# Token rows normalised and split before their transposition, one gate product, gate weights spread by select products, one return step

## The chip, the cores and the metric

The kernel runs on 1 core of one Trainium2 chip. The metric is the device time of one execution in microseconds (us); lower is better. The engines of a core are TensorE (PE: products; PEld: its weight loads), VectorE (DVE), ScalarE (ACT), GpSimd (POOL) and SyncE (SP, which here only issues transfers).

## The reference, cut to what matters

64 images of 3 x 224 x 224 and 64 texts of 77 x 64 are embedded, joined and sent through one attention block and one mixture of experts:

```python
h = patches @ W_embed + b_embed + positions            # 784 patches of 8x8, 64 features
for i in range(3):                                      # grid graph: own node plus four neighbours
    hw = h @ W_gcn[i]
    h = relu(normalised_adjacency @ hw + b_gcn[i])
h = concat([h @ W_out + b_out, txt], axis=1)            # 861 tokens
h = h + attn(layernorm(h))                              # 4 heads of 16; its output rounded to bfloat16 before Wo
h = h + ffn(layernorm(h))

def ffn(x):
    all_out = experts_mlp(x)                            # 4 experts: 64 -> 128 -> 64 -> 64, relu
    shared = shared_mlp(x)                              # 64 -> 64 -> 128 -> 64, relu
    gates = softmax(x @ gW + gb)                        # 4 gates
    topv, topi = top_k(gates, 2); topw = softmax(topv)
    return shared + sum(all_out[topi] * topw)
```

## The kernel before

**Tiling.** An image is 861 tokens = 7 blocks of 123 (`BLK`); `PIECES` are the first four and the last three blocks (492 and 369 columns), `HALVES` two times 432 columns. Two images make a pair: embedding and graph run per pair with both images side by side, attention and experts per image.

**Order.** Nothing is scheduled at run time. Each image and each pair is a list of steps such as `("s", g, half, kb, h)`; `spread` gives each step of a list a due time between a start and an end, in proportion to `COST`, and one unit of due time is one image. The constants `MAX`, `FINISH`, `NORM_M`, `EXPERT`, `NORM_A`, `PROJECT`, `VALUE` (even image, odd image), `GRAPH` and `PACK` (pair) place the lists against each other. All steps of 16 images, sorted by due time, make one window; each engine walks through the same sorted list and does its own part of every step, in that order, waiting on semaphores. The windows are separated by a drain of all engines. So a step that an engine can't start holds up all that stands behind it on that engine.

**Banks.** Steps in `ROTATING` take PSUM banks 0, 1, 2, 3, 6, 7 in turn. PE may fill a bank when the step six turns before has been read out of it. Banks 4 and 5 hold the attention output (`pv`).

**The steps that matter here**, for image g:
- `s` (L969, 56 an image): scores, read out by ACT as exponentials (L678). `pv` (L978, 14): probabilities times values, four products into four 32-column strips of the array.
- `mx` (L990, 56): scores the other way round, read out by DVE as row maxima (L790). `mrow` (L995, 2): maxima transposed, copied by ACT, sent to `QS` by SP (L559).
- `ln`, `ln2`, `ln3` (`a` before attention, `m` before the experts): layer norm on DVE, with the square on ACT and the power -0.5 on POOL. `ln3` writes the normed rows twice (L854, L855).
- `xt` (L1032): both copies of the normed rows transposed by PE; ACT rounds all 128 rows into `XS` (L694), then DVE subtracts the rounded value in rows 64 to 127 (L860), so that `XS` holds high part over low part. `qk`, `l1` (L1043), `v` and `gate` (L1054) multiply `XS` by the high and low parts of the weights.
- `gate`, `g2`, `g3`: gate values, softmax, top two, weights `GW`. In `g3` ACT repeats each weight over 64 columns (L736) into `GWW`; `wb` (L1091, 4 steps) transposes that, and DVE multiplies the hidden layer by it (L935).
- `l2` (L1083 for experts, L1081 for the shared one), `l3` (L1099), `back` (L1106, 2 steps): the result in two halves of 64 partitions goes back to token rows; DVE adds it to `H` in `OUTT` (L943), SP stores it (L565).
- `hb`: POOL adds the bias rows to `H`.
- `gw` (L1017) and `gagg` (L1026): graph layer of a pair. ACT writes the rounded `UH` (L685), DVE the rest `UL` (L809). `QKH`/`QKL` of `qk` lie in the same two tiles.
- `load` (SP, 24 transfers, L543), `xc` (POOL, L619), `embed` (L1002): a quarter of the pair's image rows. `xc` waits for the landing, and the next `load` for `xc`.
- `stack`: ACT issues 8 transfers (L717, L718) that bring q and k of image g from scratch memory into `QS` and `KS`. Due at g - 1, so once an image.

## Time and profile before

| | |
|---|---|
| median of 3 runs | 6032.26 us (6030.95 to 6034.13) |
| profiled execution, its own time | 6031.67 us |
| span from first to last instruction | 6029.7 us |
| mean granted TensorE clock | 0.914 |
| PE busy | 89% of the span |
| DVE, ACT, POOL busy | 58%, 51%, 21% |

The span is shorter than the execution's own time by 2 us. The granted clock is a share of full speed. Busy shares are means over setup (about the first 300 us) and the loop over images.

### The profile page before, as it was taken

To read this page: it belongs to the slowest core of one execution; us is meant where nothing else is said; L and a number is where in the kernel's file an instruction comes from. 1 tells how busy PE (TensorE), PEld (TensorE's weight loads), DVE (VectorE), ACT (ScalarE), POOL (GpSimd) and SP (SyncE) were. 2 spreads that over 40 slices of the span, in tenths; PEclk is the share of its full clock that TensorE was granted. 3 is DMA by queue.
4 is the path that set the end of the run, shared out by engine and by line. 5 is a ranking of instruction groups with operands and counts; after the bars stand their busy time and mean duration, and the time that the engine had idled before them with its cause. 6 is when DMAs were issued, how large, how long until landed. Compare 5 with 4: busy or idle time off the path is not lost.

```text
span 6029.7 us, 88160 instructions
## 1 busy us (share of the span) xinstructions
PE 5341.6 (89%) x30542; PEld 3460.2 (57%) x30542; DVE 3515.4 (58%) x7398; ACT 3046.5 (51%) x6161; POOL 1255.9 (21%) x1168
## 2 busy tenths in 40 slices
PE   4488999899989898999889999989998999989997
PEld 3355665556556555665556666555665555656654
DVE  2356565666555666665566665566655566656563
ACT  0044555555555555455555455555555455555555
POOL 1111221221221222122122122122122122122212
PEclk8689999998998999999998998999999899999988
DMA  1443234324334323323323323333433433332320
GB/s 36 67 68 65 50 57 71 61 52 71 56 46 71 63 52 70 57 53 63 69 50 66 57 51 65 68 58 59 70 50 53 69 58 58 71 52 50 55 39 5
DMA packets 331182, 347.37 MB, mean 58 GB/s; under 512 B 108778, under 2 KB 280938, under 8 KB 330730
## 3 DMA queue, kind: packets, MB, share of 16 engines
q1 hardware_dynamic: 289770, 228.36, 17.6%
q10 hardware_dynamic: 40960, 113.28, 15.3%
q8 instruction: 248, 4.06, 0.3%
q14 instruction: 204, 1.67, 0.1%
HBM read 269.85 MB, written 70.73 MB: 56 GB/s over the span
## 4 chain that ended last, share of the span: by engine, by line
PE 55%; DVE 15%; DMA 9%; ACT 8%; issue 5%; ACTq 4%; SPq 1%; POOL 1%; POOLq 0%; DVEq 0%
PE ps L978 10%; PE ps L990 9%; PE ps L1026 9%; PE ps L969 7%; DVE neg_max_halves L790 7%; DMA k_stack<-qk_scratch 6%; DMA image_rows<-in_x 3%; PE ps L1043 3%; ACT probs L678 3%; PE ps L1083 3%; PE ps L1054 3%; PE ps L1099 3%; ACTq L717 2%; ACTq L718 2%; PE ps L1002 2%
## 5 line engine op out<-in xcount | busy, mean ns | idle before, releaser
L790 DVE TENSOR_REDUCE neg_max_halves<-ps 123x1 f32<-123x432 f32 (+1 forms) x3584 | 2016.9, 599 | 775.3 <-PE ps L990 762.6
L678 ACT ACTIVATE probs<-ps 123x432 f32<-123x432 f32 x3584 | 1727.9, 532 | 621.8 <-PE ps L969 607.1
L990 PE MATMUL ps<-k_stack,q_stack 96*123 96x432 f32 x3584 | 1373.2, 415 | 86.1 <-DMA k_stack<-qk_scratch 53.2
L969 PE MATMUL ps<-q_stack,k_stack 97*123 97x432 f32 x3584 | 1341.8, 416 | 63.4 <-SPq L583 24.8
L978 PE MATMUL ps<-probs,v_and_one 123*32 123x432 f32 x7168 | 908.6, 581 | 170.7 <-ACT probs L678 167.0
L990 PEld LDWEIGHTS ps<-k_stack,q_stack 96*123 96x123 f32 x3584 | 652.5, 192 | 692.7 <-issue 515.3
L969 PEld LDWEIGHTS ps<-q_stack,k_stack 97*123 97x123 f32 x3584 | 684.6, 199 | 427.5 <-issue 285.0
L1026 PE MATMUL ps<-adjacency,parts_hi 112*128 112x392 f32 x1344 | 513.4, 382 | 8.4 <-DVE parts_lo L809 4.4
L1026 PE MATMUL ps<-adjacency,parts_lo 112*128 112x392 f32 x1344 | 496.9, 370 | 0.0
L690 ACT ACTIVATE nodes_T<-nodes_T,plain_w 128x392 f32<-128x392 f32 x192 | 119.5, 623 | 699.7 <-DVE nodes_T L827 699.7
L749 ACT ACTIVATE hidden<-ps,plain_w 128x432 f32<-128x432 f32 x640 | 380.8, 620 | 93.8 <-PE ps L1043 92.8
L978 PEld LDWEIGHTS ps<-probs,v_and_one 123*32 123x32 f32 x7168 | 147.0, 112 | 427.1 <-ACT probs L678 230.5
L827 DVE TENSOR_TENSOR nodes_T<-ps,dinv_row 128x392 f32<-128x392 f32 x192 | 108.8, 567 | 485.9 <-PE ps L1026 485.9
L635 POOL TENSOR_TENSOR ln_stats_a<-ln_stats_a,minus_half 123x7 f32<-123x7 f32 x64 | 94.6, 1478 | 1355.8 <-DVE ln_stats_a L848 1355.8
L631 POOL TENSOR_TENSOR nodes_T<-nodes_T,dinv_row 128x392 f32<-128x392 f32 x128 | 136.6, 1067 | 959.3 <-ACT nodes_T L690 959.3
L619 POOL COPY patch_columns<-image_rows 96x392 f32<-96x392 f32 x256 | 237.8, 957 | 392.1 <-DMA image_rows<-in_x 374.1
L755 ACT ACTIVATE hidden<-ps,plain_w 128x492 f32<-128x492 f32 (+1 forms) x384 | 238.4, 621 | 142.4 <-PE ps L1081 127.8
L1026 PEld LDWEIGHTS ps<-adjacency,parts_hi 112*128 112x128 f32 x1344 | 283.7, 211 | 45.1 <-issue 40.4
L644 POOL TENSOR_TENSOR tokens<-tokens,bias_rows 123x448 f32<-123x448 f32 x64 | 73.4, 1147 | 1125.7 <-DVE gate_weights L928 1125.7
L809 DVE TENSOR_TENSOR parts_lo<-ps,parts_hi 112x512 fp32r<-112x512 f32 x192 | 119.8, 625 | 308.6 <-ACT parts_hi L685 308.6
L648 POOL TENSOR_TENSOR tokens<-tokens,moe_T 123x448 f32<-123x448 f32 x256 | 293.1, 1145 | 20.1
L685 ACT ACTIVATE parts_hi<-ps 112x512 fp32r<-112x512 f32 x192 | 106.3, 554 | 364.5 <-PE ps L1017 229.7
(147 smaller groups left out, 7256.9 us busy)
## 6 DMA issues: line engine op xcount, KB each, us to landing
q_stack<-qk_scratch ACTq DMA_DIRECT2D x256, 216.0 KB, 9.4
k_stack<-qk_scratch ACTq DMA_DIRECT2D x256, 216.0 KB, 10.7
image_rows<-in_x SPq DMA_DIRECT2D x768, 49.0 KB
image_rows<-in_x SPq DMA_DIRECT2D x768, 48.8 KB
image_rows<-in_x SPq DMA_DIRECT2D x768, 48.6 KB
image_rows<-in_x SPq DMA_DIRECT2D x768, 48.3 KB
qk_scratch<-parts_hi SPq DMA_DIRECT2D x64, 432.0 KB, 2.5
qk_scratch<-parts_lo SPq DMA_DIRECT2D x64, 432.0 KB, 3.5
```

The lines of the kernel that those rows point to most:

```text
L619: pool.tensor_copy(XCB[:, b, :, :].rearrange("p g (i j) -> p g i j", j=GRID), src).then_inc(xc_done, 1)
L648: ins = pool.tensor_tensor(hb, hb, TMP[:, :, :], ALU.add)
L678: act.activation(P[:, unit % 2, h, :], T[0:BLK, 0:HW], ACT.Exp, scale=SCALE).then_inc(free[r], 1)
L749: act.activation(H1[e % 3][:, c0:c0 + cn], T[:, 0:cn], ACT.Relu, bias=bias).then_inc(free[r], 1)
L755: act.activation(H2[j][:, c0:c0 + cn], T[:, 0:cn], ACT.Relu, bias=bias).then_inc(free[r], 1)
L790: v.tensor_reduce(NM[:, qb * HEADS + h, half:half + 1], T[0:BLK, 0:keys], AX.X, ALU.max, negate=True).then_inc(free[r], 1)
L969: mm = pe.matmul(T[0:BLK, 0:cn], KS[:, g % 2, h, kb * BLK:(kb + 1) * BLK], QS[:, g % 2, h, c0:c0 + cn], start=True, stop=True)
L978: pm = pe.matmul(acc[32 * h:32 * h + 32, half, 0:HW], VV[:, g % 2, kb, h, :], P[:, slot, h, :], start=kb == 0, stop=kb == NB - 1, tile_pos ...
L990: mm = pe.matmul(T[0:BLK, 0:cn], QS[0:SHIFT_ROW, g % 2, h, qb * BLK:(qb + 1) * BLK], KS[0:SHIFT_ROW, g % 2, h, c0:c0 + cn], start=True, st ...
L1026: mm = pe.matmul(T[:, 0:GHALF], part[:, k, :], adj[:, k, half * GHALF:(half + 1) * GHALF], start=k == 0 and part is UH, stop=k == NG - 1 a ...
L1043: mm = pe.matmul(T[:, 0:cn], wsplit(part, name, e, cols), XS[which][:, c0:c0 + cn], start=part is WH, stop=part is WL)
L1054: mm = pe.matmul(T[0:BLK, k * cols:(k + 1) * cols], XS[which][:, k * BLK:(k + 1) * BLK], wsplit(part, "v" if kind == "v" else "gW"), start ...
```

## The change

- `ln3` writes one normed copy, then its rounded high part and the low part into `XHL`, both on DVE and token-major. `xt` transposes `XHL` by a plain product with the rounded unit matrix `ident_r` (124 columns a block, `PITCH`), and ACT alone reads the bank out. The DVE part of `xt` is gone. One `XN` serves both norms; `ln3` waits for the last `xt`.
- `mrow` is a plain product with `ident_r` too.
- `gate` multiplies each block once by the 8 columns `gsplit` (high and low part of the gate weights side by side); DVE adds the two halves.
- `g3` no longer uses ACT. DVE splits the weights into three bfloat16 parts `GP` (5 small operations); a new step `wt` transposes them (7 transpositions in bfloat16 into 12 partitions), ACT copies them to `GT` in rows 96 to 107, and each `wb` is one product of the 12-row matrix `select` with `GT`, in the array rows from 96.
- `back` is one step: 4 transpositions of all 128 partitions, two additions of DVE in place in `H`, and the store goes out of `H`. `wo` of image g now waits for the store of image g - 2; there is a semaphore for even and one for odd images.
- The two `l2` steps of a pair of experts share one due time, and so do the four `wb` steps, so that they stand side by side in the order.
- All placing constants are new. Setup makes `ident_r`, `gsplit`, `select` and clears `OT2`.

```diff
-COST = {"s": 1, "pv": 4, "mx": 1, "embed": 5, "gw": 5, "gagg": 12, "xt": 4, "qk": 2, "v": 7, "gate": 7, "l1": 2,
-        "l2": 4, "wb": 4, "l3": 12, "ot": 4, "obt": 2, "wo": 6, "back": 2, "mrow": 4}
+COST = {"s": 1, "pv": 4, "mx": 1, "embed": 5, "gw": 5, "gagg": 12, "xt": 2, "qk": 2, "v": 7, "gate": 4, "l1": 2,
+        "l2": 4, "wt": 2, "wb": 1, "l3": 12, "ot": 4, "obt": 2, "wo": 6, "back": 4, "mrow": 2}
...
-                4: [("l2", g, 1, 0), ("l2", g, 1, 1)]}[e]
-    return out + [("wb", g, 0, 0), ("l2", g, 2, 0), ("wb", g, 0, 1), ("l2", g, 2, 1), ("wb", g, 1, 0), ("wb", g, 1, 1),
-                  ("wait", 1), ("l3", g), ("wait", 1), ("back", g, 0), ("back", g, 1)]
-MAX = ((-0.804, 0.046), (-0.666, 0.05))
-FINISH = ((0.986, 1.13), (0.995, 1.13))
-NORM_M = ((1.131, 1.265), (1.15, 1.27))
-EXPERT = ((1.357, 2.01), (1.29, 1.974))
-NORM_A = ((-1.38, -1.233), (-1.9, -1.82))
-PROJECT = ((-1.247, -1.114), (-1.76, -1.666))
-VALUE = (-0.968, -0.96)
-GRAPH = (-2.04, -1.484)
-PACK = (-3.7, -3.2, -2.653, -2.19)
-LOAD_LEAD, EMBED_LAG = 0.292, 0.07
+        out += {0: [("g2", g)], 1: [("g3", g)], 2: [[("l2", g, 0, 0), ("l2", g, 0, 1)], ("hb", g)], 3: [],
+                4: [[("l2", g, 1, 0), ("l2", g, 1, 1)]]}[e]
+    return out + [("wt", g), ("l2", g, 2, 0), ("l2", g, 2, 1),
+                  [("wb", g, 0, 0), ("wb", g, 0, 1), ("wb", g, 1, 0), ("wb", g, 1, 1)], ("wait", 1), ("l3", g), ("wait", 1), ("back", g)]
+MAX = ((-0.816, -0.01), (-0.723, 0.05))
+FINISH = ((0.994, 1.13), (1.003, 1.13))
+NORM_M = ((1.131, 1.265), (1.2, 1.258))
+EXPERT = ((1.357, 1.964), (1.301, 1.99))
+NORM_A = ((-1.38, -1.245), (-1.613, -1.533))
+PROJECT = ((-1.247, -1.114), (-1.425, -1.289))
+VALUE = (-0.978, -1.013)
+GRAPH = (-2.077, -1.521)
+PACK = (-3.956, -3.348, -2.807, -2.314)
+LOAD_LEAD, EMBED_LAG = 0.138, 0.193
...
+                        sp.dma_start(dst, H[:, :, st[1] % 2, :]).then_inc(out_dma[st[1] % 2], 16)
...
-                        act.activation(XS[st[2]][:, c0:c0 + cn], T[:, 0:cn], ACT.Copy).then_inc(xt_hi, 1)
+                        act.activation(blocked(XS[st[2]][:, c0:c0 + cn]), pitched(T[:, :], cn), ACT.Copy).then_inc(free[r], 1)
...
-                    elif kind == "g3":
-                        counted(act, g_weight, nth, st)
-                        counted(act, out_dma, ranks(steps, lambda s: s[0] == "back" and s[2] == 1), ("back", st[1] - 1, 1), 16)
-                        act.activation(GWW[:, :, :, :], GW[:, :, :].unsqueeze(3).to_broadcast([BLK, NB, EXPERTS, HID]),
-                                       ACT.Copy).then_inc(g_wide, 1)
+                        act.activation(XN[:, :, 1, :], XN[:, :, 0, :], ACT.Square).then_inc(squared, 1)
+                    elif kind == "wt":
+                        act.wait_ge(full[r], n)
+                        act.activation(GT[:, 0:TOKENS].rearrange("p (k n) -> p k n", n=BLK),
+                                       T.bitcast(BF16)[0:3 * EXPERTS, 0:NB * (BLK + 1)].rearrange("p (k n) -> p k n", k=NB)[:, :, 0:BLK],
+                                       ACT.Copy).then_inc(free[r], 1)
...
-                        v.tensor_tensor(XN[which][:, :, 1, :], XN[which][:, :, 0, :], rstd, ALU.mult)
-                        v.tensor_tensor(XN[which][:, :, 0, :], XN[which][:, :, 0, :], rstd, ALU.mult).then_inc(normed, 1)
-                    elif kind == "xt":
-                        v.wait_ge(xt_hi, hi_no[st])
-                        tile = XS[st[2]]
-                        c0, cn = PIECES[st[3]]
-                        v.tensor_tensor(tile[64:128, c0:c0 + cn], T[64:128, 0:cn],
-                                        tile[64:128, c0:c0 + cn].bitcast(F32), ALU.subtract).then_inc(free[r], 1)
+                        filled(v, turn, xt_last[st])
+                        settle(v.tensor_tensor(XN[:, :, 0, :], XN[:, :, 0, :], rstd, ALU.mult))
+                        settle(v.tensor_copy(XHL[:, :, 0, :], XN[:, :, 0, :]))
+                        v.tensor_tensor(XHL[:, :, 1, :], XN[:, :, 0, :], XHL[:, :, 0, :].bitcast(F32),
+                                        ALU.subtract).then_inc(normed, 1)
...
+                        counted(v, out_dma[g % 2], out_no[g % 2], ("back", g - 2), 16)
...
-                        ins = v.tensor_tensor(GZ[:, 0, :, :], T[0:BLK, 0:NB * EXPERTS].rearrange("p (k e) -> p k e", e=EXPERTS),
-                                              row("gb", 0, EXPERTS).unsqueeze(1).to_broadcast(sh), ALU.add)
-                        ins.then_inc(free[r], 1)
+                        t8 = T[0:BLK, 0:NB * 2 * EXPERTS].rearrange("p (k a e) -> p k a e", a=2, e=EXPERTS)
+                        settle(v.tensor_tensor(GZ[:, 0, :, :], t8[:, :, 0, :],
+                                               row("gb", 0, EXPERTS).unsqueeze(1).to_broadcast(sh), ALU.add))
+                        v.tensor_tensor(GZ[:, 0, :, :], t8[:, :, 1, :], GZ[:, 0, :, :], ALU.add).then_inc(free[r], 1)
...
+                        v.wait_ge(g_weight, nth[st])
+                        filled(v, turn, ("wt", st[1] - 1))
+                        settle(v.tensor_copy(GP[:, :, 0, :], GW[:, :, :]))
+                        settle(v.tensor_tensor(GR[:, 0, :, :], GW[:, :, :], GP[:, :, 0, :], ALU.subtract))
+                        settle(v.tensor_copy(GP[:, :, 1, :], GR[:, 0, :, :]))
+                        settle(v.tensor_tensor(GR[:, 1, :, :], GR[:, 0, :, :], GP[:, :, 1, :], ALU.subtract))
+                        v.tensor_copy(GP[:, :, 2, :], GR[:, 1, :, :]).then_inc(g_parts, 1)
...
+                        t4 = T[0:BLK, 0:4 * 128].rearrange("p (k t f) -> p k t f", t=2, f=HID)
+                        v.tensor_tensor(H[:, 0:4, g % 2, :], t4[:, :, 0, :], H[:, 0:4, g % 2, :], ALU.add)
+                        v.tensor_tensor(H[:, 4:NB, g % 2, :], t4[:, 0:3, 1, :], H[:, 4:NB, g % 2, :], ALU.add
+                                        ).then_inc(free[r], 1)
...
-                            mm = pe.transpose(T[0:HEADS, at * BLK:(at + 1) * BLK],
-                                              NMM[:, k * HEADS:(k + 1) * HEADS], ident[0:BLK, 0:BLK])
+                            mm = pe.matmul(T[0:HEADS, at * PITCH:(at + 1) * PITCH], NMM[:, k * HEADS:(k + 1) * HEADS],
+                                           ident_r[0:BLK, 0:BLK + 1], start=True, stop=True)
...
-                            src = XN[st[2]][:, k, :, :].rearrange("p a f -> p (a f)")
-                            mm = pe.transpose(T[:, at * BLK:(at + 1) * BLK], src, ident[0:BLK, 0:BLK])
+                            src = XHL[:, k, :, :].rearrange("p a f -> p (a f)")
+                            mm = pe.matmul(T[:, at * PITCH:(at + 1) * PITCH], src, ident_r[0:BLK, 0:BLK + 1],
+                                           start=True, stop=True)
...
+                            x_ = XS[which][:, k * BLK:(k + 1) * BLK]
+                            if kind == "gate":
+                                mm = pe.matmul(T[0:BLK, k * 2 * EXPERTS:(k + 1) * 2 * EXPERTS], x_, gsplit[:, :],
+                                               start=True, stop=True)
...
+                        counted(pe, g_parts, nth, ("g3", st[1]))
+                        for k in range(NB):
+                            mm = pe.transpose(T.bitcast(BF16)[0:3 * EXPERTS, k * (BLK + 1):k * (BLK + 1) + BLK],
+                                              GP[:, k, :, :].rearrange("p a e -> p (a e)"), ident_bf[0:BLK, 0:BLK])
                     elif kind == "wb":
                         _, g, j, t = st
+                        c0, cn = PIECES[t]
                         if (j, t) == (0, 0):
-                            counted(pe, g_wide, nth, ("g3", g))
-                        for k, at in blocks_of(t):
-                            src = GWW[:, k, 2 * j:2 * j + 2, :].rearrange("p a f -> p (a f)")
-                            mm = pe.transpose(T[:, at * BLK:(at + 1) * BLK], src, ident[0:BLK, 0:BLK])
+                            emptied(pe, turn, ("wt", g))
+                        mm = pe.matmul(T[:, 0:cn], select[:, 2 * j:2 * j + 2, :].rearrange("p a f -> p (a f)"),
+                                       GT[:, c0:c0 + cn], start=True, stop=True, tile_position=(SEL_ROW, 0))
...
+                        emptied(pe, turn, ("l3", st[1]))
+                        for k in range(4):
+                            mm = pe.transpose(T[0:BLK, k * 128:(k + 1) * 128], OT2[:, k * BLK:(k + 1) * BLK], ident[:, :])
```

## Rows read from the trace of the kernel before

**Rows 1.** The page: span, and busy time of each engine.
```profile
span 6029.7 us, 88160 instructions
PE 5341.6 (89%) x30542; PEld 3460.2 (57%) x30542; DVE 3515.4 (58%) x7398; ACT 3046.5 (51%) x6161; POOL 1255.9 (21%) x1168
```

**Rows 2.** Windows: length, busy us (instructions) of each engine, PEclk, DMA share, GB/s.
```profile
1500.00:4500.00 3000.00, 2732.66 (x15765) 1769.25 (x15765) 1811.55 (x3819) 1588.02 (x3214) 651.19 (x608) 0.93 0.34 59
2619.38:2627.14 7.76, 7.76 (x28) 7.31 (x28) 1.16 (x3) 1.04 (x3) 0.00 (x0) 0.50 1.07 126
```

**Rows 3.** Waits: who waited for whom, us in total, times, longest.
```profile
PE ps L978 <- ACT probs L678: 167.0, 233, 2.6
...
PE ps L1054 <- DVE parts_lo L809: 122.0, 30, 5.2
...
PE ps L990 <- DMA k_stack<-qk_scratch: 53.2, 22, 28.6
```

**Rows 4.** Timeline, two pieces a pair apart: start, length, what [idle before].
```profile
2618.25 0.49 ACT L685 ACTIVATE parts_hi<-ps 112x384 fp32r<-112x384 f32 x1 [4.28 <-issue]
...
2619.38 0.41 PE L1054 MATMUL ps<-split_hi,x_stack_attn 128*123 128x64 f32 x1 [4.15 <-DVE parts_lo L809]
...
2796.90 0.41 PE L1054 MATMUL ps<-split_hi,x_stack_attn 128*123 128x64 f32 x1 [4.16 <-DVE parts_lo L809]
```

**Rows 5.** Window of L1054 alone: fourteen gate products of one image.
```profile
3011.15:3012.65 1.50, 1.50 (x14) 1.48 (x13) 1.00 0.58 85
```

**Rows 6.** Timeline of PE around three `wb` transpositions.
```profile
3046.61 0.46 PE L990 MATMUL ps<-k_stack,q_stack 96*123 96x432 f32 x1
3046.90 0.48 PE L1091 MATMUL ps<-ident,gate_weights_wide 123*128 123x123 f32 x3
3047.14 0.44 PE L990 MATMUL ps<-k_stack,q_stack 96*123 96x432 f32 x1
```

**Rows 7.** Timeline of PE around three `back` and three `ot` transpositions.
```profile
3063.57 0.46 PE L990 MATMUL ps<-k_stack,q_stack 96*123 96x432 f32 x1
3063.95 0.53 PE L1106 MATMUL ps<-ident,moe_T 64*123 64x64 f32 x3
3064.41 0.65 PE L990 MATMUL ps<-k_stack,q_stack 96*123 96x432 f32 x2
3064.91 0.49 PE L1061 MATMUL ps<-ident,attn_T 128*123 128x128 f32 x3
```

**Rows 8.** Timeline of PE: products in bfloat16, and transpositions into 4 partitions.
```profile
56.69 1.65 PE L394 MATMUL ps<-onehot_dst,onehot_src 126*112 126x392 bf16 x9
...
2628.10 0.57 PE L1066 MATMUL ps<-ident_bf,attn_bf 123*64 123x123 bf16 x7
...
3067.43 0.48 PE L995 MATMUL ps<-ident,neg_max 123*4 123x123 f32 x3 [1.20 <-DVE neg_max L797]
3067.67 0.86 PE L969 MATMUL ps<-q_stack,k_stack 97*123 97x432 f32 x3
```

**Rows 9.** Groups by form, DVE and ACT: count, busy us, mean ns, idle.
```profile
L790 DVE TENSOR_REDUCE neg_max_halves<-ps 123x1 f32<-123x432 f32 x1792 | 1078.3, 602 | 493.6 <-PE ps L990 487.1
...
L855 DVE TENSOR_TENSOR normed_twice_m<-normed_twice_m,ln_stats_m 123x448 f32<-123x448 f32 x64 | 39.6, 619 | 0.0
...
L860 DVE TENSOR_TENSOR x_stack_moe<-ps,x_stack_moe 64x369 fp32r<-64x369 f32 x64 | 35.0, 547 | 18.5 <-ACT x_stack_moe L694 17.6
...
L928 DVE TENSOR_TENSOR gate_weights<-gate_vals,gate_sums 123x28 f32<-123x28 f32 x64 | 12.1, 189 | 2.2
...
L678 ACT ACTIVATE probs<-ps 123x432 f32<-123x432 f32 x3584 | 1727.9, 532 | 621.8 <-PE ps L969 607.1 <-issue 4.0
```

**Rows 10.** Timeline of SP and POOL: two loads, the packing after one.
```profile
2617.16 25.53 SPq L543 DMA_DIRECT2D image_rows<-in_x  x24
...
2722.16 14.09 SPq L543 DMA_DIRECT2D image_rows<-in_x  x24
...
2738.66 1.77 POOL L619 COPY patch_columns<-image_rows 96x392 f32<-96x392 f32 x2 [11.29 <-DMA image_rows<-in_x]
```

More of the change, by code:

```diff
@@ L31 @@
 BLK = 123
+PITCH = BLK + 1
 NB = TOKENS // BLK
@@ L48 @@
 SHIFT_ROW = 96
+SEL_ROW = 96
 HW = 432
@@ L195, in windows @@
     return out
-ROTATING = ("s", "embed", "gw", "gagg", "mx", "mrow", "ot", "obt", "wo", "xt", "qk", "v", "gate", "l1", "l2", "wb", "l3",
+ROTATING = ("s", "embed", "gw", "gagg", "mx", "mrow", "ot", "obt", "wo", "xt", "qk", "v", "gate", "l1", "l2", "wt", "wb", "l3",
             "back")
```

114 lines of the change are left out of this document (64 added, 50 removed).

## The prediction

> **What bounds the kernel now.** I read the page first: PE is busy 89% of the span, the next engine 58% [rows 1]. In the loop PE is busy 2732.7 of 3000 us at a granted clock of 0.93 [rows 2], so PE work saved there is time saved, unless another engine sets the pace in that stretch. A pair of images takes 2796.90 - 2619.38 = 177.5 us [rows 4], an image 88.8 us, which turns due times into us. The missing 9% is not spread evenly. The list of waits names a PE wait of 122.0 us in 30 times at the first `v` product, one a pair [rows 3]. The timeline shows its chain [rows 4]: ACT issues the 8 transfers of `stack` and is away 4.28 us ("issue"), only then evicts the second half of `gw` (L685), DVE follows, and `v`, which takes the bank of that `gw` six turns later, starts 4.15 us late. After it come 28 products, 14 of `v` and 14 of `gagg`, in 7.76 us at clock 0.50 [rows 2], which is the 1.2 GHz level after an idle PE. Two smaller stops a pair stand behind the other `stack`: `pv` waits for exponentials that queue behind it on ACT, and the first `mx` for the landing of `k_stack` [rows 3].
>
> **PE work, per image at full clock.** Because products overlap, I take ends, not lengths. Fourteen gate products take 1.50 us, 0.107 each, though only 4 columns stream: their 123-column weight load sets it [rows 5]. Three `wb` transpositions end 3047.38 - 3047.07 = 0.31 us after the product before, 0.105 each, with a run-out of 0.48 - 0.31 = 0.17 us, and the next 432-column product ends 0.20 us later [rows 6].
> - `gate`: 14 products become 7: -0.75 us.
> - `back`: 7 x 0.107 becomes 4 x 0.11 (three `ot` transpositions, the same shape, end 0.34 us apart from what precedes [rows 7]): -0.31.
> - `wb`: 14 x 0.105 = 1.47 goes. Bfloat16 streams 392 columns in (1.65 - 0.17) / 9 = 0.164 us, and seven small transpositions take (0.57 - 0.17) / 7 = 0.057 each [rows 8]. So 2 x (0.21 + 0.155) = 0.73 for the four products and 0.40 for `wt`: -0.34.
> - `mrow`: 7 transpositions at 0.105 become products of 124 columns with 4 weight columns. At the 0.20 us for 432 columns that is 0.057: -0.34. `xt`: 14 products with 128 weight columns, 0.107 x 128/123 = 0.111 against 0.105: +0.08. No row shows this rounded format streaming 65 to 391 columns. One bound is 0.057; the other is 0.22, two passes of 0.11 as an unrounded 128-column product would take by the `ot` price. Then `mrow` and `xt` cost 21 x 0.115 = 2.4 us more instead of saving 0.26. I take the lower price, as gate, `s` and `mx` are all in this format and none runs in two passes.
> - Array shape. `back` works on 64 partitions. Three of its transpositions end 0.45 us after the product before and the two products behind end 0.58 later [rows 7]: 0.45 - 3 x 0.107 = 0.13 us going in, 0.58 - 0.40 = 0.18 coming out. `pv`, `embed`, `obt`, `l2` of the experts and `l3` are strips as well. I laid out the due times of both versions for one window of 16 images: before, 24.0 entries into a strip shape and 21.9 returns an image; after, 22.5 and 19.0. Gone are two `back` and two of four `l2` entries, added one `wt`, one `wb` (the four stand together) and 1.5 `mrow`. That is 1.5 x 0.13 + 2.9 x 0.18 = -0.72.
>
> The Trainium skill, page TensorEngine Tiling (Array Packing), section Tiling Modes, says that changing the mode drains TensorE; it speaks against the new `wt`, `wb` and `mrow`, and for the grouped `l2` and `back`. The trace agrees for `back` (0.31 us in all), but `mrow` with 4 output columns shows nothing of it now: after its three transpositions three products end in 0.62 us, their plain price [rows 8]. By the rule `mrow` as a plain product pays from now on; by that row it would not, and the array-shape term would be 2.5 x 0.13 + 3.9 x 0.18 = -1.03, 20 us less in all. I take it as paying.
>
> The sum is -0.75 - 0.31 - 0.34 - 0.34 + 0.08 - 0.72 = -2.38 us an image, -152 us for 64.
>
> **The order.** In the new due times `gw` of the first layer falls at 1.953 and 1.967 of a pair, `v` at 1.987, and `stack` at 2.0. So the eviction that PE waited for now stands ahead of the 8 issues on ACT. Behind them on PE come two `gagg` (5.0 us), two `ot` and four `s`, about 6.6 us of work (a 392-column product is 0.18 us at the rate of `mx`), before `pv` needs exponentials that ACT has after 4.28 + 3 x 0.53 = 5.9 us [rows 4, 9]. The stop of 122.0 us goes, and with it the low clock: 7.76 us at 0.50 would be 3.88, 30 times 116 us. Together -238 us. The other `stack` keeps its place at 1.0 and its stops: the first `mx` is due 1 us earlier (1.184) but waits for the same landing. `ln` and its square move away from there, which frees `pv` sooner, only for `mx` to wait longer: zero.
>
> **DVE and ACT.** DVE loses four `xt` subtractions, the shorter 0.55 us, 2.4 us an image, and gains a copy in `ln3` (between 0.19 and 0.62 by [rows 9]; I take 0.35) twice, one small operation in `gate` and five in `g3` at 0.19: about -0.6. ACT loses the wide copy and gains the narrow one. Neither mean matters; the place does. `ln`, `ln2`, `ln3` of the odd image are now due at 1.387 to 1.44, in between `gate`, `g2` and `g3` of the even one. From 1.387 to 1.515, 11.4 us, DVE has 5 large operations of 0.62 (3.1), a copy (0.35), 23 small ones of 0.19 (4.4) and 9 maxima of 0.60 (5.4): 13.2 us [rows 9]. Before, a stretch as long held 11 small ones and 11 maxima, 8.7 us. Behind them on DVE stand maxima whose banks PE needs. I charge 2 us a pair, +64. Four `wb` side by side leave four reads of some 0.6 us to DVE within 0.73 us of PE; PE has two banks beyond them. I charge 0.5 us an image, +32; zero and 1.5 us are the bounds.
>
> **Transfers.** `load` now comes 0.138 (12.3 us) ahead of `xc`, before 0.292 (25.9). The packing starts 2738.66 - 2722.16 = 16.5 us after the first issue when it must wait [rows 10], so POOL will stand in `xc` some 4 us in each. Behind it on POOL is the power of `ln2` (due 0.665, `xc` 0.652), and DVE's `ln3` at 0.710 waits for that: 1 us, hidden by the banks. `load` at 1.906 stands ahead of `mrow`'s transfers of 1.963 on SP; the row is needed at 2.5. The store out of `H` is waited for by `wo` 100 us later. Setup gets six more small operations on DVE and one clearing on POOL, under 2 us, left out.
>
> The profiled execution took 6031.7 us, within 1 us of the median, so 6031.7 - 152 - 238 + 64 + 32 = 5738 us.
>
> **Rivals.**
> - *Only the products.* ACT's 4.28 us of issuing are still there, and my margin behind them was 6.6 against 5.9 us. If the stop only moves from `v` to `pv`, the order brings nothing: 6032 - 152 = 5880. For it: all engines walk one order, and what ACT holds up must be somewhere. Against it: 5 us of that margin are `gagg`, which nobody has to empty in between.
> - *Slow narrow products.* At 0.22 us each, 2.4 + 0.26 us an image more, +170: 5908. For it: no row in between. Against it: `v` streams 64 columns at the gate's pace.
> - *More than forecast.* DVE's stretch is absorbed, no charge of 96 us, and `pv` and `mx` behind the other `stack` wait 2 to 3 us a pair less: about 5560.
> - *Slower: the late load.* The load that shares its time with `stack` takes 25.53 us only to issue, the other 14.09 [rows 10]. If all did, with packing 2.4 us behind the last issue as in [rows 10] and its two copies of 1.77 us, POOL would reach the power 29.7 us after the first issue, while `ln3` is due 0.196 of an image, 17.4 us, after it. DVE would stand over 12 us, PE some 11 after its banks are full: 32 pairs x 11 = 352, 5738 + 352 = 6090. It decides from 9.2 us a pair on, a packing that starts 26 us after the first issue. Against it: only the first load of a pair meets `stack`, and nothing near it needs POOL.
>
> **How the numbers follow.** Forecast 0.52 (5640 to 5820), only the products 0.17, slow narrow products 0.07, more than forecast 0.12, late load 0.06, and 0.06 that several DVE stretches become the pace and it stays where it was. The range 5585 to 5910 takes in the first three and half of the fourth. A change below 0.2% (12 us) can't be told from none here: faster 0.89, same 0.04, slower 0.07.
>
> **What would show it.** Right: the wait of L1054 on `parts_lo` gone, granted clock of the loop above 0.95, gate products 7 an image at 0.107, `xt` at 0.11, `back` without the 0.31 us. Wrong: a PE wait at `pv` right behind the first `stack`; `mx` banks waited for around g3; POOL in `xc` over 10 us with DVE idle before `ln3`.

## The result, and the profile after

The changed kernel takes 6074.82 us (median of 4 runs, 6072.12 to 6078.07), the kernel before 6033.19 beside it: ratio 1.0068, 95% interval 1.0051 to 1.0086. It is slower, where 5738 us and a range of 5585 to 5910 were forecast.

The page after, its first lines and the granted clock by slices, against [rows 1]:

```profile
span 6072.3 us, 86871 instructions
PE 5299.8 (87%) x29710; PEld 3405.8 (56%) x29710; DVE 3564.0 (59%) x7660; ACT 3028.8 (50%) x6161; POOL 1232.6 (20%) x1169
PEclk8689999888998888998888898888998989899888
```

PE has 832 instructions and 42 us of busy time less, and DVE, which should have lost work, has 49 us more. The windows of [rows 2] again, with two stretches of one pair (length, busy us of PE, PEld, DVE, ACT, POOL, granted clock, DMA share, GB/s):

```profile
1500.00:4500.00 3000.00, 2664.81 (x15128) 1710.64 (x15127) 1805.73 (x3885) 1552.77 (x3163) 618.59 (x591) 0.90 0.37 59
2723.50:2747.20 23.70, 20.14 (x85) 11.56 (x86) 8.87 (x18) 9.19 (x20) 1.47 (x1) 0.50 0.72 92
2704.00:2721.00 17.00, 15.91 (x88) 8.66 (x88) 11.67 (x25) 7.76 (x16) 0.00 (x0) 1.00 0.18 65
```

The loop's clock is 0.90, not above 0.95 (0.93 before): behind the even `stack` (the one of the even image; its first issue is at 2719.28 in this pair) PE runs 23.7 us at 0.50, 85 instructions, where 17 us at full clock just before held 88. The list of PE's waits, against [rows 3] (us in total, times, longest):

```profile
PE ps L1043 <- POOL patch_columns L655: 154.2, 22, 24.3
PE ps L1019 <- ACT probs L713: 126.8, 269, 4.7
PE ps L1031 <- DMA k_stack<-qk_scratch: 120.4, 32, 31.0
PE ps L1031 <- DVE neg_max_halves L826: 82.9, 89, 2.1
PE ps L1128 <- DVE neg_max_halves L826: 58.0, 31, 1.9
PE ps L1010 <- ACT probs L713: 34.4, 31, 2.5
PE ps L1085 <- DVE neg_max_halves L826: 31.0, 30, 1.2
```

L1043 is `embed`, L1019 `pv`, L1031 `mx`, L1128 `l2`, L1010 `s`, L1085 `qk` and `l1`. The 122.0 us at `v` are gone, and 39 of the 43.4 at `mrow`. New or far longer are three kinds of stops for a bank that DVE has not emptied (`mx`, `l2`, `qk` and `l1`), one at `s` for exponentials, and stops at `embed` for the packed image: 80.8 of the 154.2 us, in the 16 pairs from 1851 to 4589 us; before, the same wait had 76.0 us, of which 1.4 lay behind the first 300 us. The wait for `k_stack` at the first `mx` behind the even stack has grown from 53.2 us in 22 times [rows 3] to 120.4 in 32, though the stack lands no later (18.3 us behind its first issue in the median, 18.6 before). The place of `embed` in one pair, on PE, SP and POOL:

```profile
2737.91 0.69 PE L1031 MATMUL ps<-k_stack,q_stack 96*123 96x432 f32 x1 [2.96 <-DMA k_stack<-qk_scratch]
...
2757.30 1.58 PE L1043 MATMUL ps<-patch_columns,embed_w 96*64 96x196 f32 x8 [5.19 <-POOL patch_columns L655]
```

```profile
2724.51 13.73 SPq L592 DMA_DIRECT2D q_stack<-image_rows  x4
2738.43 26.46 SPq L576 DMA_DIRECT2D image_rows<-in_x  x39
```

```profile
2755.46 1.69 POOL L655 COPY patch_columns<-image_rows 96x392 f32<-96x392 f32 x2 [18.63 <-DMA image_rows<-in_x]
```

The four row transfers of `mrow` take 13.73 us on SP beside the stack, 7.49 us at the same place of the kernel before, and the third load of the pair stands behind them: it starts 19.2 us after the stack's first issue, 12.0 before the change. POOL stands 18.63 us for it, and PE 5.19.

Where DVE is late, at g3, two of the five small operations are not small (groups by form, and the place itself on DVE and POOL):

```profile
L967 DVE TENSOR_TENSOR gate_weight_rest<-gate_weights,gate_weight_parts 123x28 f32<-123x28 f32 x64 | 64.4, 1006 | 2.2
L969 DVE TENSOR_TENSOR gate_weight_rest<-gate_weight_rest,gate_weight_parts 123x28 f32<-123x28 f32 x64 | 49.6, 776 | 2.2
```

```profile
2773.54 1.01 DVE L967 TENSOR_TENSOR gate_weight_rest<-gate_weights,gate_weight_parts 123x28 f32<-123x28 f32 x1
2774.59 0.18 DVE L968 CAST gate_weight_parts<-gate_weight_rest 123x28 bf16<-123x28 f32 x1
2774.80 0.77 DVE L969 TENSOR_TENSOR gate_weight_rest<-gate_weight_rest,gate_weight_parts 123x28 f32<-123x28 f32 x1
```

```profile
2773.37 1.14 POOL L679 TENSOR_TENSOR tokens<-tokens,bias_rows 123x448 f32<-123x448 f32 x1 [8.79 <-DVE gate_weights L962]
2774.59 0.95 POOL L681 TENSOR_TENSOR moe_T<-gate_weights,bias_rows 123x448 f32<-123x448 f32 x1
```

```profile
2776.36 0.84 PE L1128 MATMUL ps<-hidden,plain_w 128*64 128x369 f32 x4 [1.88 <-DVE neg_max_halves L826]
```

L967 ends at 2774.55, when POOL's first `hb` operation ends (2774.51), and L969 at 2775.57 with the second (2775.54). `hb` and these five start from the same event, the gate weights.

**One balance for all kernels.** From PE's records and the granted clock I split each profiled execution in three: PE's busy time with what lies at 0.50 counted at half ("work"), the other half of that time ("half clock"), and time in which PE stands after its first instruction ("idle"). Some 39 us lie around them. The times in these tables are medians, the three columns are of the one profiled execution: where that one lay off the median (old_ops_new_times 6443 against 6386, filled_mx_stop 6008 against 6034, hb_behind_parts 5948 against 5967), they add up to its time. The second line is my forecast in these terms (work -152; half clock -116; idle -122 + 64 + 32).

```
kernel                 time   work  half clock  idle
before                 6033   4943    399       651
forecast of after      5738   4791    283       625
after                  6075   4752    548       734
```

Work fell by 191 us, 39 more than forecast. The miss is half clock, 265 us over the forecast, and idle, 109.

Where the half clock lies, as time at 0.50 in a pair (mean of the pairs):

```
from the stack's first issue     before   after
even stack, 0 to 31 us            15.3    21.5
even stack, 31 to 62 us            0.4    11.8
odd stack, 0 to 31 us              9.4     1.5
```

The stretch from 31 to 62 us holds the stop at `embed` and, at its end, the stop at `l2`.

### The profile page after: what moved, and what is told of

It reads as the page before. It is cut to its first block, busy times and chain, and to the rows that moved or that the text cites. A ratio compares the mean times of both kernels' runs of the same rounds, so it can differ in the third digit from the quotient of the medians.

```text
span 6072.3 us, 86871 instructions
## 1 busy us (share of the span) xinstructions
PE 5299.8 (87%) x29710; PEld 3405.8 (56%) x29710; DVE 3564.0 (59%) x7660; ACT 3028.8 (50%) x6161; POOL 1232.6 (20%) x1169
## 4 chain that ended last, share of the span: by engine, by line
PE 50%; DVE 16%; ACT 6%; DMA 6%; SPq 5%; issue 5%; ACTq 4%; POOL 2%; DVEq 0%; POOLq 0%
PE ps L1019 11%; PE ps L1031 10%; DVE neg_max_halves L826 6%; PE ps L1067 6%; PE ps L1010 6%; ACT probs L713 4%; PE ps L1085 3%; DMA k_stack<-qk_scratch 3%; SPq L576 3%; DMA image_rows<-in_x 3%; PE ps L1149 3%; PE ps L1128 2%; SPq L592 2%; ACTq L753 2%; ACTq L754 2%
## 5 line engine op out<-in xcount | busy, mean ns | idle before, releaser
L1031 PE MATMUL ps<-k_stack,q_stack 96*123 96x432 f32 x3584 | 1432.4, 432 | 208.7 <-DMA k_stack<-qk_scratch 120.4
L1010 PE MATMUL ps<-q_stack,k_stack 97*123 97x432 f32 x3584 | 1356.6, 418 | 75.0 <-ACT probs L713 34.4
L1031 PEld LDWEIGHTS ps<-k_stack,q_stack 96*123 96x123 f32 x3584 | 696.2, 205 | 854.9 <-issue 645.0
L1019 PE MATMUL ps<-probs,v_and_one 123*32 123x432 f32 x7168 | 974.2, 618 | 127.6 <-ACT probs L713 126.8
L1010 PEld LDWEIGHTS ps<-q_stack,k_stack 97*123 97x123 f32 x3584 | 726.8, 208 | 305.6 <-issue 106.2
L1067 PE MATMUL ps<-adjacency,parts_hi 112*128 112x392 f32 x1344 | 474.9, 353 | 26.3 <-DVE parts_lo L845 26.3
L1067 PE MATMUL ps<-adjacency,parts_lo 112*128 112x392 f32 x1344 | 462.0, 344 | 0.0
L1019 PEld LDWEIGHTS ps<-probs,v_and_one 123*32 123x32 f32 x7168 | 153.4, 114 | 429.9 <-issue 220.1
L671 POOL TENSOR_TENSOR ln_stats_m<-ln_stats_m,minus_half 123x7 f32<-123x7 f32 x64 | 94.6, 1478 | 1316.8 <-DVE ln_stats_m L884 1316.8
L1067 PEld LDWEIGHTS ps<-adjacency,parts_hi 112*128 112x128 f32 x1344 | 257.4, 191 | 60.9 <-issue 59.4
L1085 PE MATMUL ps<-x_stack_moe,split_hi 128*128 128x432 f32 x640 | 263.0, 411 | 31.0 <-DVE neg_max_halves L826 31.0
L922 DVE TENSOR_TENSOR tokens<-ps,tokens_next 123x448 f32<-123x448 f32 x64 | 40.0, 624 | 401.2 <-PE ps L1117 401.2
```

Of the source, the lines that this page charges most:

```text
L1010: mm = pe.matmul(T[0:BLK, 0:cn], KS[:, g % 2, h, kb * BLK:(kb + 1) * BLK], QS[:, g % 2, h, c0:c0 + cn], start=True, stop=True)
L1019: pm = pe.matmul(acc[32 * h:32 * h + 32, half, 0:HW], VV[:, g % 2, kb, h, :], P[:, slot, h, :], start=kb == 0, stop=kb == NB - 1, tile_pos ...
L1031: mm = pe.matmul(T[0:BLK, 0:cn], QS[0:SHIFT_ROW, g % 2, h, qb * BLK:(qb + 1) * BLK], KS[0:SHIFT_ROW, g % 2, h, c0:c0 + cn], start=True, st ...
L1067: mm = pe.matmul(T[:, 0:GHALF], part[:, k, :], adj[:, k, half * GHALF:(half + 1) * GHALF], start=k == 0 and part is UH, stop=k == NG - 1 a ...
L1085: mm = pe.matmul(T[:, 0:cn], wsplit(part, name, e, cols), XS[which][:, c0:c0 + cn], start=part is WH, stop=part is WL)
```

## The experiments

Each was timed beside the kernel before; ratios are to that kernel's runs on the same chip. "After" is 1.0068.

**First: the operations or the order?**

new_ops_old_times: `after` with MAX to EMBED_LAG of before, and XN and XHL doubled ({"a", "m"}). COST, the grouped `l2` and the grouped `wb` stay those of after.

> All new operations, but every due time as before the change, with a second pair of buffers for the centred and the split rows, since the single pair needs the new times. Theory: the operations save what I summed and the loss sits in the new due times; then 6033 - 152 = about 5880 us, with the stop at v (some 4 us a pair) back. Rival: the operations save little or nothing, since other engines' work behind them (the parts of g3 on DVE, the split) or a price of mine is wrong; then 6000 to 6080 us.

old_ops_new_times: before, with MAX to EMBED_LAG of after.

> The operations of before (fourteen gate products, wb transposed from the wide copy, two back steps, rows split after the transposition), with the new due times of all steps, PACK, LOAD_LEAD and EMBED_LAG. Theory that the loss sits in the due times: slower than after by what the operations save, about 6075 + 150 = 6225 us, with PE waiting at embed for patch_columns and a 20 us stretch at half clock behind a stack. Rival that the operations eat the gain and the times bring it: the stop at v is gone and the time is below 6033, down to 5800 us.

load_times_old:

```diff
-PACK = (-3.956, -3.348, -2.807, -2.314)
-LOAD_LEAD, EMBED_LAG = 0.138, 0.193
+PACK = (-3.7, -3.2, -2.653, -2.19)
+LOAD_LEAD, EMBED_LAG = 0.292, 0.07
```

> After, with PACK, LOAD_LEAD and EMBED_LAG of before: loads come 26 us ahead of the packing again, embed 0.07 behind it. PE's wait of 154.2 us at embed for patch_columns should go, and with it the stretch of 7 to 14 us at half clock behind it, 4 to 6 us a pair. Theory that the late load is the largest part of the miss: 6075 - 154 - 110 = about 5810 us. Rival: the wait is slack of something else that ends at the same place (the stack's landing, POOL), and goes over to mx or gw: 6040 to 6080 us.

max_times_old:

```diff
-MAX = ((-0.816, -0.01), (-0.723, 0.05))
-VALUE = (-0.978, -1.013)
+MAX = ((-0.804, 0.046), (-0.666, 0.05))
+VALUE = (-0.968, -0.96)
```

> After, with MAX and VALUE of before: the last two mx of an image at 0.046 instead of -0.01, mrow ahead of v as before. Theory that the row transfers of mrow and the transfers of stack now collide (the four row transfers take 13.7 us of SP where they took 7.5, and load stands behind them): the half-clock stretch of 24 us a pair behind the even stack shrinks to the 10 us of before, 32 x 14 / 2 = 220 us less, and load starts 6 us earlier: about 5800 to 5900 us. Rival: the collision depends on stack alone, time as after within 20 us.

```
kernel                 time   ratio (interval)          work  half clock  idle
new_ops_old_times      6365   1.0543 (1.0521, 1.0564)   4794    767       755
old_ops_new_times      6386   1.0560 (1.0540, 1.0580)   4950    609       845
load_times_old         6171   1.0214 (1.0190, 1.0237)   4726    620       786
max_times_old          6210   1.0284 (1.0264, 1.0303)   4773    647       747
```

All four are slower than both kernels. The work column says what the times hide: the new operations take 149 us of work away (4943 to 4794), the new times alone nothing (4950). But every mixture pays in half clock and idle. None of the four times lies in a range that I expected, on either side. I take it that going back with one group of times among others that moved with it makes new collisions; no run here shows which. So a whole group of times is no clean experiment here, and the next ones change single steps.

**Second: one suspected step each.**

third_load_early:

```diff
+LOAD_MORE = (0.0, 0.0, 0.075, 0.0)
-        out += [(t + PACK[q] - LOAD_LEAD, ("load", p, q)),
+        out += [(t + PACK[q] - LOAD_LEAD - LOAD_MORE[q], ("load", p, q)),
```

> After, with one load of each pair (the third quarter) issued at 0.98 of a pair instead of 1.055, ahead of the even stack and ahead of the row transfers of mrow that take 13.7 us on SP beside it. Theory: PE's stop at embed (5.2 us in the pairs that take 184 us, none in those that take 174 to 177.5) is that load standing on SP behind the row transfers; it goes, and with it the 7 to 14 us at half clock behind it: 22 pairs x 5 to 9 us, 110 to 200 us less, 5870 to 5960. Rival: the transfers that run beside the stack make the stack land later, the stop goes over to mx: 6050 to 6100 us.

filled_mx_stop (adds work that nobody reads):

```diff
                         if (qb, h, half) == (0, 0, 0):
+                            if g % 2 == 0:
+                                for _w in range(16):
+                                    pe.matmul(T[:, 0:HW], ident_r[:, :], WH[:, 0:HW], start=True, stop=True)
                             counted(pe, stack_dma, nth, ("stack", g), STACK_LOADS)
```

> After, with 16 products of 432 columns of constants into the bank of the first mx of each even image, ahead of its wait for the stack: work that nobody needs, 2.9 us at full clock, where PE stands 3.0 us anyway. Theory that idle PE costs by its clock: the 9 us at half clock behind the landing become full, 32 x 4.7 = 150 us less, 5925 us, although PE has more work. Rival: the clock stays low, the filling runs at 0.50 (5.8 us) and the landing is missed by up to 3 us: 6075 to 6170 us.

before_new_graph (in the kernel before):

```diff
-VALUE = (-0.968, -0.96)
-GRAPH = (-2.04, -1.484)
+VALUE = (-0.978, -1.013)
+GRAPH = (-2.077, -1.521)
```

> Before, with GRAPH and VALUE of after alone: gw of the first layer and v move ahead of stack. Theory of the prediction: the stop of 4.15 us at v and the half clock behind it go, 238 us less, 5795 us. Rival: what the ACT queue holds up for 4.3 us turns up at the next product that needs an eviction (pv, s), and the half clock with it: 6000 to 6060 us.

l2_apart:

```diff
-2: [[("l2", g, 0, 0), ("l2", g, 0, 1)], ("hb", g)], 3: [], 4: [[("l2", g, 1, 0), ("l2", g, 1, 1)]]
+2: [("l2", g, 0, 0), ("l2", g, 0, 1), ("hb", g)], 3: [], 4: [("l2", g, 1, 0), ("l2", g, 1, 1)]
```

> After, with the two l2 of an expert pair spread as before instead of side by side (same bound steps, one more entry into and one more return from the strip shape in two places an image). Theory that the grouping pays by the array shape: 2 x (0.13 + 0.18) = 0.62 us an image, 40 us slower, 6115 us. Rival: the group costs the stop of 1.9 us a pair at l2 (58 us in 31 times) and the half clock behind it; apart it is 60 to 110 us faster, 5965 to 6015 us.

```
kernel                 time   ratio (interval)          work  half clock  idle
third_load_early       5991   0.9925 (0.9907, 0.9944)   4759    502       687
filled_mx_stop         6034   0.9994 (0.9972, 1.0016)   4886    416       666
before_new_graph       5948   0.9853 (0.9837, 0.9870)   4948    377       583
l2_apart               6038   0.9992 (0.9979, 1.0005)   4783    511       712
```

The load alone is worth 84 us, less than the 110 expected at least; PE's wait at `embed` falls from 154.2 to 83.1 us. The row transfers are back at 3.02 us, and the load in front of the stack pays for it (26.98 us for 24 issues) where nobody waits:

```profile
2708.82 26.98 SPq L577 DMA_DIRECT2D image_rows<-in_x  x24
2735.84 3.02 SPq L593 DMA_DIRECT2D q_stack<-image_rows  x4
```

The filled stop has 134 us more work and is still 41 us faster than after by the medians: half clock fell by 132 and idle by 68 in its profiled execution, which was 66 us faster. 150 us were expected. The new times of `gw` and `v` in the kernel before bring 89 us, not 238, and so lie between theory and rival: the stop at `v` is gone, but PE's waits at `pv` for exponentials grow from 167.0 us [rows 3] to 201.4, a new one of 33.6 us stands at `mx`, and the half clock falls by only 22 us in place of 116:

```profile
PE ps L978 <- ACT probs L678: 201.4, 196, 4.9
...
PE ps L990 <- DMA k_stack<-qk_scratch: 44.0, 21, 28.1
...
PE ps L990 <- ACT hidden L749: 33.6, 31, 1.3
```

l2 apart costs 31 us of work, near what the array shape was priced at (40), and is 37 us faster all the same. The wait of 58.0 us at `l2` is gone from the list, but as much stands at `s` for the same maxima, so the stop moved rather than went; the gain is half clock (37 us) and idle (22):

```profile
PE ps L1010 <- DVE neg_max_halves L826: 59.2, 33, 1.9
```

**Third: DVE beside POOL.**

hb_behind_parts:

```diff
-                        counted(pool, g_weight, nth, ("g3", g))
+                        counted(pool, g_parts, nth, ("g3", g))
```

> After, with POOL's hb released by the last of the five part operations of g3 on DVE instead of by the gate weights before them. In after the two subtractions among the five take 1.01 and 0.78 us where I priced 0.19, in all 64 images, and each ends with the POOL operation that runs beside it. Theory: a DVE operation with two inputs in SBUF stands while POOL works; apart they take 0.19, DVE gets 1.4 us an image back, and the stop of 1.9 us at l2 (58 us in 31 times) goes: 60 to 110 us less, 5965 to 6015 us. Rival: the two subtractions are slow by their mixed types, whatever POOL does; the rows stay at 1.01 and 0.78 and the time at 6075.

hb_and_load: this edit and that of third_load_early.

> Both: hb behind the parts, and the third load at 0.98 of a pair. Theory that the late load and the held DVE are separate causes of the miss: their gains add, 5991 minus 60 to 110 us, 5880 to 5930. Rival that both are slack of one pace (the landing of the stack, ACT): no more than 20 us below the 5991 of the load alone.

hb_load_l2_apart: and that of l2_apart.

> As hb_and_load, with the l2 of an expert pair spread as before. Theory that the grouping only cost because DVE was held there: with DVE free the group pays by the array shape, so apart is 20 to 40 us slower than hb_and_load. Rival: two banks at once are late anyway, apart stays 20 to 40 us faster, as it was in after (6038 against 6075).

hb_load_filled: hb_and_load and the filling of filled_mx_stop.

> As hb_and_load, with the 16 products of constants ahead of the first mx of even images. Theory that the half clock behind the stack's landing is still paid: about 40 to 80 us below hb_and_load, the granted clock 0.02 to 0.03 higher. Rival: without the later stops the clock comes back by itself and the filling is only work: 0 to 60 us slower.

```
kernel                 time   ratio (interval)          work  half clock  idle
hb_behind_parts        5967   0.9889 (0.9868, 0.9910)   4765    474       669
hb_and_load            5881   0.9728 (0.9704, 0.9751)   4771    456       630
hb_load_l2_apart       5827   0.9648 (0.9632, 0.9664)   4803    390       592
hb_load_filled         5850   0.9690 (0.9674, 0.9706)   4894    361       552
```

The two subtractions, by form, in hb_behind_parts:

```profile
L969 DVE TENSOR_TENSOR gate_weight_rest<-gate_weight_rest,gate_weight_parts 123x28 f32<-123x28 f32 x64 | 12.0, 187 | 2.2
L967 DVE TENSOR_TENSOR gate_weight_rest<-gate_weights,gate_weight_parts 123x28 f32<-123x28 f32 x64 | 12.0, 187 | 2.2
```

The same operations on the same types take 187 ns, so it was not the types: they had stood beside POOL. That is 1.41 us of DVE an image, 90 us in all, and 108 us of time. Of PE's waits for DVE those at `mx` and `l2` shrink, from 82.9 and 58.0 us:

```profile
PE ps L1031 <- DVE neg_max_halves L826: 37.7, 51, 2.1
...
PE ps L1128 <- DVE neg_max_halves L826: 14.4, 31, 0.5
```

The 31.0 us at `l1` and `qk` stay as they are, so they have another cause, and the wait for `k_stack` grows from 120.4 to 148.2 us.

The load's 84 and these add (5881, within what was expected). The expectation of hb_load_l2_apart fell: with DVE free, l2 apart is 54 us faster still. By the ratios to the kernel before it is 0.8% here and was 0.8% in l2_apart, so the held DVE was not what the grouping cost. hb_load_filled is 32 us faster than hb_and_load, less than the 40 to 80 expected, though its clock did rise by 0.02.

**Fourth: what was still open.**

old_times_hb: new_ops_old_times with hb_behind_parts' edit.

> As new_ops_old_times (6365 us), with hb behind the parts. Theory: the held DVE subtractions are what makes the operations cost at any due times; then at least the 108 us of hb_behind_parts, more since the stops here are more: 6150 to 6260. If it were the whole of it, 5880. Rival: the old due times place other work of DVE and PE badly for the new operations (stops at mrow, l1, mx, half clock), and hb is a small part: 6300 to 6360.

before_stack_on_sp: in the kernel before, the `stack` branch moved word for word from ACT to SP.

> Before, with the 8 transfers of each stack issued by SP instead of ACT at the same place of the order. Theory of the prediction: the stop at v (122.0 us and the half clock behind it) is ACT's 4.28 us of issuing; it goes, and so do the small stops at pv behind both stacks: 5800 to 5900 us. Rival: SP's queue then carries the stack, the row transfers and the load one behind the other, the stack or the load lands later and PE stands at mx or embed instead: 6000 to 6200 us.

apart_gate14:

```diff
-                                mm = pe.matmul(T[0:BLK, k * 2 * EXPERTS:(k + 1) * 2 * EXPERTS], x_, gsplit[:, :],
+                                for a_ in range(2):
+                                    mm = pe.matmul(T[0:BLK, (2 * k + a_) * EXPERTS:(2 * k + a_ + 1) * EXPERTS], x_,
+                                                   gsplit[:, a_ * EXPERTS:(a_ + 1) * EXPERTS],
```

> As hb_load_l2_apart (5827 us), with the gate in fourteen products of four columns again (same columns of the bank, same eviction). Theory: PE work costs its own time where no other engine's stop takes it up: 64 x 0.75 = 48 us slower, 5875. Rival that the gate's place has slack (the banks and the clock decide): within 15 us of 5827; and one that denser PE work lifts the clock: not slower at all.

apart_filled: hb_load_l2_apart with 12 filling products.

> As hb_load_l2_apart, with 12 products of constants (2.2 us at full clock) ahead of the first mx of even images. Theory: as in hb_load_filled, 20 to 40 us less, 5790 to 5805. Rival: this version's half clock behind the landing is already short, the filling makes no difference: 5820 to 5840.

old_order_new_ops: old_times_hb, and

```diff
+COST: xt 4, gate 7, wb 4, mrow 4 (as before)
+4: [("wt", g), ("l2", g, 1, 0), ("l2", g, 1, 1)]
+("wb", g, 0, 0), ("l2", g, 2, 0), ("wb", g, 0, 1), ("l2", g, 2, 1), ("wb", g, 1, 0), ("wb", g, 1, 1)
```

> As old_times_hb (6320 us), and now also the old entries of COST (mrow 4, xt 4, gate 7, wb 4, in place of 2, 2, 4, 1), l2 spread, and the four wb spread between l2 and l3 with wt ahead of the second l2 pair: the kernel before with the new operations and nothing else of its order changed. Theory: in old_times_hb the shorter costs bring mrow and others due before DVE is through (107 us of stops at mrow in 124 times, 43 before), that goes; with the operations' 152 us: 5880. Rival: the operations themselves put DVE behind (ln3's copy, two gate additions, five part operations an image), at any order; 6100 to 6300.

apart_old_graph: hb_load_l2_apart with GRAPH and VALUE of before.

> As hb_load_l2_apart (5827 us), with GRAPH and VALUE of before: the stop of 4.15 us at v behind the odd stack comes back. Theory of the prediction, by the stop and the half clock behind it: 238 us slower, 6065. By what the same edit gave in the kernel before (89 us, since part of the stop turned up at pv and the half clock moved elsewhere): 5915. Rival: the new times of the other steps already keep them clear of each other: under 30 us.

```
kernel                 time   ratio (interval)          work  half clock  idle
old_times_hb           6320   1.0465 (1.0444, 1.0485)   4782    723       768
before_stack_on_sp     6106   1.0096 (1.0071, 1.0120)   4955    287       832
apart_gate14           5852   0.9689 (0.9669, 0.9709)   4849    384       579
apart_filled           5816   0.9621 (0.9602, 0.9641)   4886    365       544
old_order_new_ops      6059   1.0045 (1.0031, 1.0059)   4825    537       657
apart_old_graph        6038   1.0001 (0.9990, 1.0013)   4791    574       634
```

old_times_hb is only 45 us faster than new_ops_old_times, where 108 at least were expected: its two subtractions are at 188 and 187 ns again, so at the old due times the held DVE is a small part of what the new operations cost, as the rival had it.

With the stack on SP the stop at `v` is gone from the list of waits, so it was ACT's issuing, and half clock falls by 112 us, close to the 116 of the forecast. But idle grows by 181: 139 us more at `mx` than in [rows 3] and 187 more at `embed` (76.0 before) take the stop's place. That load and stack now share a queue is the likely reason, as the rival had it; no row here shows it alone:

```profile
PE ps L1002 <- POOL patch_columns L632: 262.9, 35, 23.8
...
PE ps L990 <- DMA k_stack<-qk_scratch: 192.6, 32, 17.4
```

Seven gate products more an image add 46 us of work, 48 by the prediction's price, and 25 us of time, between theory and rival. The filling brings nothing that can be told in the version apart: the intervals overlap.

old_order_new_ops differs from the kernel before by the operations alone (with the later `hb` and the doubled buffers): 118 us less work, 138 us more half clock, the same idle, 23 us slower; 5880 was expected, or 6100 at least. Behind the even stack it has 23.7 us at 0.50 in the 31 us, 15.3 before: over 31 pairs 130 of the 138 us. Its stops are those of before, `v` among them; those at `pv` (203.9 us, 167.0 before) and `mrow` (70.7, 43.4 before) are longer:

```profile
PE ps L1018 <- ACT probs L712: 203.9, 295, 3.5
PE ps L1099 <- DVE parts_lo L844: 107.6, 30, 5.3
```

And apart_old_graph brings that same stop (103.9 us in 30 times) into the fast version: 210 us slower, 184 of it half clock, 42 idle, with 12 us less work. That is near the 238 of the prediction and far from the 89 in the kernel before.

## Why the prediction was wrong, by its own steps

**PE work per image: right, and right by its parts.** -152 us was forecast; 149 was measured with the new operations at the old times, 191 with everything (where the other 42 come from was not traced). By the ends of equal products at full clock the trace after gives 0.111 us for `xt`, 0.057 for `mrow` and 0.107 for the gate, 0.109 for `back` without an entry, 0.21 and 0.16 for the bfloat16 `wb`. The slow narrow products did not come. Grouping l2 saved 32 us of work of the 40 that its share of the array-shape term gives. One slip in that term: the entries named there (four gone, three and a half added) make 0.5 fewer, not the 1.5 that were counted and priced, 0.13 us an image; no run settles which is right.

**What work saved is worth: the step that the sum left out.** I took PE work for time. In the old order 118 us less of it became +23: half clock took 138 us, nearly all of them behind the even stack. Where there were fewer stops, 46 us of work made 25 us of time, about half. That stops which stay give back what work saves between them is my reading; old_order_new_ops also has other work on DVE and ACT, and no run parts the two.

**The order, -238 us: the mechanism right, the size true only where no other stop is near.** The stop at `v` was ACT's issuing and it left, and its low clock with it: 7.9 us less at 0.50 behind the odd stack of each pair, worth 122 us in 31 pairs, where 116 were forecast. Alone, in the kernel before, the edit is worth 89 us; in the version with the other stops mended 210. That other stops near it make this difference is argued, not shown. The even stack, "zero" in the prediction, is the step of this term that failed: the wait for `k_stack` grew by 67 us, and the time at 0.50 in the 31 us behind its first issue from 15.3 to 21.5 us a pair, which is 96 us of half clock. The next 31 us, with the stops at `embed` and `l2`, went from 0.4 to 11.8 us a pair, another 177. The filled stop shows that the first of these stretches is paid (41 us net of 134 us of useless work). Why PE stands longer for a stack that lands at the same time was not tried; the growth stays with the mends below (149.4 us in hb_load_l2_apart).

**DVE and ACT: the failed step.** "Five in `g3` at 0.19": two took 1.01 and 0.78, as they ran beside POOL's `hb`. I read their price from a row [rows 9] where POOL was not at work, and did not ask what the gate weights release beside them. Waits for banks around g3 had been named as the sign of a wrong forecast, and they came: 58.0 us at `l2` and 82.9 at `mx`, of which 14.4 and 37.7 are left without the collision. Undone, 108 us. The l2 pair, which I counted only as array shape, gave 37 and then 54 us when it was taken apart; that it takes two banks at once is a guess at the reason, which no run shows. My 64 + 32 covered neither.

The Trainium skill, page SBUF — State Buffer, section Who interferes with whom, says that a VectorE instruction with two SBUF inputs contends with a GpSimd instruction that reads SBUF and that the one issued later blocks until the first is through; the trace agrees: 1.01 and 0.78 us against 0.187, each to the end of the POOL operation that had started before it, while the copy between them, with one input, took its 0.18 us beside POOL.

**Transfers: the second failed step.** The load at 1.906 did no harm, but the one that cost was the third, at 1.055 of a pair. I had POOL stand "some 4 us" for each load; for the third it stood 13.6 to 20.6 us in 16 pairs, about 10 us in the kernel before. I looked at its lead ahead of the packing and not at what it stands behind on SP, the row transfers that take 13.7 us beside the stack. 84 us. The rival "the late load" had the late landing, but another path and price: it had DVE stand over 12 us in `ln3` for POOL's power, and that wait is never over 2.5 us (65.7 us in 33 times); PE met the load at `embed`, with 5 us in the pairs that had it, not 11.

**The sum.** From after, the three mends give 6075 - 248 = 5827 us, 89 above the forecast and inside its range; what remains is half clock, 390 us where 283 was forecast, with work 12 above and idle 33 below it. So the miss of 337 us is 108 for the held DVE, 86 for the load on top of it (84 by itself), 54 for the pairs of l2, and 89 that stayed, all of it half clock by this balance.

**Open:** why the new operations at the old times, with the new costs and groups (6320), cost 261 us more than with the old costs and places (6059). Half clock (186 us) and idle (111) carry it, and PE waits 107 us at `mrow` there against 71; which of the moved steps does it was not tried apart. Open too is why load_times_old and max_times_old came out slower, why l2 apart is faster, and what makes the longer wait for `k_stack`.

## What to carry to other kernels

Price a small operation from a row where the same neighbours are at work, and ask what else the event before it releases. A transfer's due time says little: look at what stands before it on its queue. Where the clock of TensorE falls at short stops, take the stops out first: here TensorE work saved brought nothing in the order with its stops, and half its length in the version with fewer. A kernel like this is to be judged by work, half clock and idle apart, since the total hides that one pays for the other. The version with the three mends is 3.5% faster than before.

## What the runs showed of the hardware

- In the loop of after (1500 to 4500 us) the clock fell to 0.50 in 52 stretches of 3.4 to 23.9 us. The one at 2723.3 came behind stops of 0.62 us (at 2715.6) and 0.86 us (at 2722.8) and lasted 23.9 us, with PE busy 85% of it and one stop of 2.96 us inside. Useless products in that stop raised the mean granted clock from 0.885 to 0.915. The Trainium skill, page TensorE: Matmul & The Clock Gate, section A second HAM failure mode: psum-queue depth-cycling, tells of a kernel in which frequent small pauses between groups of products make the clock swing; the trace agrees, with these 52 stretches.
- The length of a pair, from one even stack's first issue to the next, favours few values in some of the kernels: in after 20 of 31 pairs lie within 0.7 us of 174.0, 177.6, 180.9 or 184.3 us; in before 15 lie between 177.0 and 178.3 us and none at the other three; apart_old_graph, with 152 us less work than before, again has 16 of its 31 between 177.0 and 178.3. In hb_load_l2_apart, the fastest but one, only 3 of 31 lie near the four values of after. No run here shows why.
- Four row transfers of 1.5 to 1.9 KB took 13.7 us to issue in after, from 5.2 us behind a stack's first issue on, 7.5 us in before, from 4.3 us on, and 3.0 us in third_load_early, once the load stood in front of them.
- A DVE operation of 123x28 with both inputs in SBUF took 1.01 and 0.78 us beside a POOL operation of 123x448, 0.187 us without one.
